# Two layers of self- and cross-attention on one core: when a group's row maxima are computed, and where its keys wait

## The reference

```python
h1 = ln(x);  x = attn(h1, h1,      20 heads of 16) + x      # self:  512 queries x  512 keys
h2 = ln(x);  x = attn(h2, context, 20 heads of 16) + x      # cross: 512 queries x 1601 keys
h3 = ln(x);  a, g = split(h3 @ ff_w1 + ff_b1)               # 320 -> 2 x 1280
x  = (a * gelu(g)) @ ff_w2 + ff_b2 + x
# attn: softmax(q k^T / 4) v per head, then a projection
```

## Time and profile before

| what | value |
|---|---|
| time, median of 3 runs | 3695.53 us (3688.76 to 3696.15) |
| time of the profiled execution | 3690.11 us |
| its span, first to last instruction | 3688.3 us |
| mean granted TensorE clock | 0.931 of full |
| busy: PE, DVE, ACT, POOL | 88%, 56%, 54%, 17% of the span |

### The profile page before, as it was taken

How to read it: one execution, slowest core, us unless ns; L and a number is a source line. 1 busy time by engine, 2 the same in 40 slices (tenths; PEclk the granted TensorE clock), 3 DMA queues, 4 the chain that set the end, 5 groups by cost and what they waited for, 6 DMA issues and landing times.

```text
span 3688.3 us, 43767 instructions
## 1 busy us (share of the span) xinstructions
PE 3235.1 (88%) x16320; PEld 1493.1 (40%) x16320; DVE 2080.8 (56%) x2565; ACT 1989.5 (54%) x3806; POOL 620.7 (17%) x676
## 2 busy tenths in 40 slices
PE   5887888998899989999899988999988988887877
PEld 2333333343353434534344433544344534433435
DVE  5555565665555765557555655556755665455511
ACT  1543565656655656456664566545665566354531
POOL 2231121203102120112202132021210031001001
PEclk8987988999998999999999888999999999998989
DMA  6434335333433243332443445323333243222202
GB/s 156 140 90 97 95 89 141 89 82 88 126 89 108 68 107 94 95 96 53 130 107 87 120 119 147 97 90 72 92 92 87 46 101 90 63 43 47 69 24 71
DMA packets 194515, 340.88 MB, mean 92 GB/s; under 512 B 19384, under 2 KB 101696, under 8 KB 193024
## 3 DMA queue, kind: packets, MB, share of 16 engines
q1 hardware_dynamic: 194304, 338.08, 35.5%
HBM read 202.29 MB, written 114.75 MB: 86 GB/s over the span
## 4 chain that ended last, share of the span: by engine, by line
PE 60%; DVE 14%; DMA 11%; ACT 6%; POOL 3%; issue 3%; SPq 3%; DVEq 0%; ACTq 0%; POOLq 0%
DVE mx L933 12%; PE pr L1124 11%; PE po L1141 11%; PE pd L1105 7%; PE pf L1049 5%; PE pf L996 5%; PE pf L1060 5%; DMA QS<-scr_q 5%; PE pf L1019 3%; PE pf L1037 3%; ACT ET L852 3%; PE pf L1028 3%; DMA scr_k<-HS 2%; PE pf L1052 2%; DMA raw<-ff_w_dram 1%
## 5 line engine op out<-in xcount | busy, mean ns | idle before, releaser
L852 ACT ACTIVATE ET<-pr 128x512 f32<-128x512 f32 (+1 forms) x2720 | 1478.1, 596 | 1372.5 <-PE pr L1124 1356.8
L933 DVE TENSOR_REDUCE mx<-pd 128x2 f32<-128x804 f32 (+2 forms) x1600 | 1569.4, 1033 | 1004.2 <-PE pd L1105 1001.7
L1124 PE MATMUL pr<-QS,KS 64*128 64x512 f32 (+1 forms) x2720 | 871.0, 514 | 86.6 <-ACT ET L852 84.1
L1105 PE MATMUL pd<-KS,QS 64*128 64x400 f32 (+2 forms) x3200 | 636.2, 396 | 160.0 <-DVE mx L933 85.4
L1141 PE MATMUL po<-ET,V 128*32 128x512 f32 (+2 forms) x5440 | 770.2, 640 | 1.2 <-ACT OU L858 1.2
L1124 PEld LDWEIGHTS pr<-QS,KS 64*128 64x128 f32 (+1 forms) x2720 | 337.4, 189 | 962.7 <-ACT ET L852 648.5
L1105 PEld LDWEIGHTS pd<-KS,QS 64*128 64x128 f32 x3200 | 361.1, 197 | 302.9 <-DVE mx L933 194.0
L743 POOL TENSOR_TENSOR HS<-uT,HS 128x512 fp32r<-128x512 f32 (+4 forms) x168 | 189.9, 1131 | 762.5 <-ACT uT L816 762.5
L759 POOL TENSOR_TENSOR OA<-OA,DEN 128x512 f32<-128x512 f32 (+1 forms) x48 | 60.8, 1267 | 1259.5 <-DVE DEN L941 1259.5
L1049 PE MATMUL pf<-HS,WS 128*128 128x512 f32 x730 | 217.7, 430 | 50.1 <-DVE uT L926 17.8
L1019 PE MATMUL pf<-cT,w_kv 96*128 96x400 f32 (+3 forms) x384 | 168.3, 564 | 31.5 <-ACT uT L816 30.6
(11 more groups left out here) (82 smaller groups left out, 2186.0 us busy)
## 6 DMA issues: line engine op xcount, KB each, us to landing
WS<-parts SPq DMA_DIRECT2D x160, 320.0 KB, 2.9
KS<-scr_k SPq DMA_DIRECT2D x80, 600.8 KB, 10.6
QS<-scr_q SPq DMA_DIRECT2D x80, 512.0 KB, 10.2
scr_k<-HS SPq DMA_DIRECT2D x144, 200.0 KB
scr_q<-HS SPq DMA_DIRECT2D x96, 256.0 KB
KS<-scr_k SPq DMA_DIRECT2D x80, 192.0 KB, 3.7
scr_k<-HS SPq DMA_DIRECT2D x48, 256.0 KB
OA<-OU SPq DMA_DIRECT2D x320, 32.0 KB
```

What stands on the lines that cost most here:

```text
L852: activation(ET[0:q.rows[k], s % 2, 2 * pair + e, :], pr[e][0:q.rows[k], :], ACT.Exp).then_inc(score_free, 1)
L933: v.reduce_max(mx[:, t, 2 * p:2 * p + 2, c], pd[no % 2][:, :, 0:cols], AX_X).then_inc(unit_free, 1)
L1105: ins = mm(pd[no % 2][:, e, 0:cols], queries[:, t * P:(t + 1) * P], keys, start=True, stop=True)
L1124: mm(pr[e][0:m, :], keys, queries, start=True, stop=True).then_inc(score_ready, 1)
```

## The change

It is one new plan for the units, with four parts around it.

1. **Units.** Outside the self-only stretches a group's units stand only on beats with `b % 4 == 2`, place three of a step. S units may spread over 16 beats in place of 8, so four places; C units have their own chain of `_turn`, so that S and C units may stand at one place. Per pair of 17 steps, 40 units: before, they stood at 17 places with two units and 6 with one. After, by the rule of the diff, the 510 steps of the mixed stretch have 262 places with two C units, 66 with three C, 117 with two S and then two C, 2 with two S and three C, 1 with two S, and 62 with none; the last 130 steps have 64 places with four C units, 8 with three, 3 with two, 55 with none. The first C group has four places with eight units; before it had eight with four.
2. **Slots and maxima by kind.** S groups stay in one slot of `QS`, C groups alternate between the other two; `mx` has a tile for each kind. A C group is loaded 16 beats earlier than before in the mixed stretch (with the end of the C group two before it), not together with an S group. Its first unit stands at least 11 beats behind the load, an S group's at least 8 (10 in effect); before it was 7 (8 in effect) for both. In the C-only stretch the load stays and the first unit stands 14 beats behind it, before it was 8.
3. **Self-only stretches.** Their units stay. Moves, reciprocals and division come earlier: 6, 9 to 12 and 13 beats behind a group's end. Fills of the second stretch begin up to one place earlier.
4. **Order of the last passes.** Fills of phase c = 6 are dealt by `deal_by_steps` (one stretch per step, two short ones at both odd places); `ff2` of pass 5 moves to the start of the last phase, where the norms `n3` are mixed with the values, and the last gate takes four `a` fills together, before three.
5. **Waits.** `turn_maxima` waits for all units issued before it, and the first unit behind a turn waits for the copies of that turn.

```diff
     elif c == N - 1:
-        first, rest = gate(c - 1, 3)
-        seq = places("v2b", c) + mixed(places("o2", c - 1), []) + places("n3", c - 1) + places("t3", c - 1)
-        seq += places("g", c - 1) + [first] + rest
+        first, rest = gate(c - 1, 4)
+        seq = places("ff2", c - 2) + places("o2", c - 1) + mixed(places("v2b", c), places("n3", c - 1))
+        seq += places("t3", c - 1) + places("g", c - 1) + [first] + rest
...
+        if i is None:
+
+            seq = [p for p in seq if p[0] != "ff2"]
...
+            _last = {s: max([p.end for p in GROUPS if p.slot == s], default=0) for s in range(SLOTS)}
+            _own = [p.slot for p in GROUPS if p.kind == _kind and (_kind == "C" or p.step0 >= 2 * G * TT)]
+            if _kind == "C" and _crosses >= 2:
+                _slot = _own[-2]
+            elif _kind == "S" and _own:
+                _slot = _own[-1]
+            else:
+                _slot = min(_last, key=_last.get)
...
-    _over = [p.n for p in GROUPS[:_q.n] if p.n <= _q.n - RING or p.shares_keys(_q)]
+    _over = [p.n for p in GROUPS[:_q.n] if p.slot == _q.slot or p.shares_keys(_q)]
...
 COPY, MOVE, INVERT, DIVIDE = 5, 8, (14, 15, 16, 17), 18
+
+MOVE_ALONE, INVERT_ALONE, DIVIDE_ALONE = 6, (9, 10, 11, 12), 13
...
+SHORT = ("t1", "t2", "t3", "tc")
+
+
+def deal_by_steps(stretches, steps):
+
+
+    slots, kinds = [], []
+    for stretch in stretches:
+        works = [p[0] for p in stretch if p[0] in STAGE]
+        if works and works[0] in SHORT and slots and kinds[-1] == works[0] and len(slots[-1]) == 1:
+            slots[-1].append(stretch)
+        elif slots and kinds[-1] is None:
+            slots[-1][-1] = slots[-1][-1] + stretch
+            kinds[-1] = works[0] if works else None
+        else:
+            slots.append([stretch])
+            kinds.append(works[0] if works else None)
+    assert len(slots) <= len(steps)
+    for k, slot in enumerate(slots):
+        for n, stretch in enumerate(slot):
+            PLACES.setdefault(4 * steps[k * len(steps) // len(slots)] + 1 + 2 * n, []).extend(stretch)
...
-        _behind = [b for b in _odd if b > 4 * _from + DIVIDE]
+        _behind = [b for b in _odd if b > 4 * _from + DIVIDE_ALONE + 2]
...
+    elif _c == N - 2:
+        deal_by_steps(_all, range(_from + 1, _to))
...
-    _from = max(_at + 7, _free, 0)
-
+
+    _alone = _q.end <= 2 * G * TT
+    _from = max(_at + (8 if _q.kind == "S" else 11), _turn[_q.kind] + 3, 0)
+    if _alone:
+        _from = max(_at + 7, _turn["S"] + 2, 0)
     _lag = 5 if 4 * _q.step0 - _from >= 24 else 3
-    _to = 4 * _q.step0 - _lag - (4 if _lag == 5 else 2)
+    _to = 4 * _q.step0 - _lag - 2
     if _q.kind == "S":
-        _to = min(_to, _from + 8)
-    _beats = [b for b in range(_from, _to) if b % 2 == 0]
+        _to = min(_to, _from + (8 if _alone else 16))
+    _beats = [b for b in range(_from, _to) if (b % 2 == 0 if _alone else b % 4 == 2) and b + 1 not in TURN_AT and b - 1 not in TURN_AT]
...
-        mx = sb("mx", [P, TT, HG, len(CHUNKS)])
+        mx = {"S": sb("mx1", [P, TT, HG, 1]), "C": sb("mx2", [P, TT, HG, len(CHUNKS)])}
...
-                if u == 0 and q.n:
-                    pe.wait_ge(max_copied, HG * q.n)
+                elif TURNS_BEFORE[no] > TURNS_BEFORE[no - 1]:
+                    pe.wait_ge(max_copied, HG * TURNS_BEFORE[no])
...
+            def turn_maxima(q, units):
+
+                pe.wait_ge(unit_free, units)
                 pe.wait_ge(max_steps, 3 * (q.n + 1))
```

More of the change, by code:

```diff
@@ L121, in stages_beside @@
             first, rest = gate(c - 1, 4)
-            seq += behind[:2] + places("t3", c - 1) + places("g", c - 1) + [first] + rest
-            behind = behind[2:]
+            seq += behind[:1] + places("t3", c - 1) + places("g", c - 1) + [first] + rest
+            behind = behind[1:]
+        if i is None:
+            seq = [p for p in seq if p[0] != "ff2"]
         if c + 3 < N:
-            behind = mixed(behind[:2], places("n1", c + 3)) + behind[2:]
+            behind = places("n1", c + 3) + behind
             behind += places("t1", c + 3) + places("q1", c + 3) + places("k1", c + 3)
@@ L136, with __init__ @@
 class Group:
-    def __init__(self, n, kind, i, g, step0, unit0, at):
+    def __init__(self, n, kind, i, g, step0, at, slot, uses):
         self.n, self.kind, self.i, self.g = n, kind, i, g
@@ L167 @@
                 _at, _selves = JP + T * (_selves % 3) if _c is None else 2 * JP, _selves + 1
-            GROUPS.append(Group(len(GROUPS), _kind, _pass, _g, _q.end if _q else 0,
-                                _q.unit0 + len(_q.units) if _q else 0, _at))
+            GROUPS.append(Group(len(GROUPS), _kind, _pass, _g, _q.end if _q else 0, _at, _slot,
+                                sum(p.slot == _slot for p in GROUPS)))
     PHASE_STEPS.append((_from, GROUPS[-1].end))
 STEP = [(q, k) for q in GROUPS for k in range(q.kt)]
-UNIT = [(q, u) for q in GROUPS for u in range(len(q.units))]
 LAST_OF = {(q.kind, q.i): q for q in GROUPS}
@@ L288, in split_for @@
     return max(fills, key=lambda p: SPLIT[p])
-STAGE_AT, UNITS_AT, TURN_AT, = {}, [0] * BEATS, {}
-_free = 0
+STAGE_AT, UNITS_AT, TURN_AT = {}, {b: [] for b in range(BEATS)}, {FIRST_BEAT: GROUPS[0]}
+_turn = {"S": FIRST_BEAT, "C": FIRST_BEAT}
 for _q in GROUPS:
@@ L462, in blocks_kernel @@
         gelu_done = sem("gelu_done")
-        staged = [sem(f"staged{r}") for r in range(RING)]
+        staged = [sem(f"staged{r}") for r in range(SLOTS)]
         unit_ready = sem("unit_ready")
@@ L693, in _ @@
                     set_scratch("q2", 1)
-                if ended(beat, MOVE):
-                    move_rows(ended(beat, MOVE))
+                if ended(beat, MOVE, MOVE_ALONE):
+                    move_rows(ended(beat, MOVE, MOVE_ALONE))
             sp.wait_ge(x_stored, 16 * B * TT)
@@ L763, in _ @@
                     beside(*p)
-                if ended_slot(beat, DIVIDE):
-                    divide(ended_slot(beat, DIVIDE))
+                if ended_slot(beat, DIVIDE, DIVIDE_ALONE):
+                    divide(ended_slot(beat, DIVIDE, DIVIDE_ALONE))
         @block.scalar
@@ L874, in _ @@
                     beside(*p)
-                if ended(beat, COPY):
-                    take_sums(ended(beat, COPY))
+                if ended(beat, COPY, COPY):
+                    take_sums(ended(beat, COPY, COPY))
         @block.vector
@@ L965, in _ @@
                     set_key_rows()
-                    for u in range(len(GROUPS[0].units)):
-                        reduce(GROUPS[0], u)
+                    for no in range(len(GROUPS[0].units)):
+                        reduce(no)
                 if beat in TURN_AT:
@@ L970, in _ @@
                 if 0 <= beat < BEATS:
[L971 to L975, removed]
+                    for no in range(UNITS_BEFORE[beat], UNITS_BEFORE[beat] + len(UNITS_AT[beat])):
+                        reduce(no)
+                for part, behind in enumerate(zip(INVERT, INVERT_ALONE)):
+                    if ended_slot(beat, *behind):
+                        invert(ended_slot(beat, *behind), part)
         @block.tensor
@@ L1149, in _ @@
                 if beat == FIRST_BEAT:
-                    for u in range(len(GROUPS[0].units)):
-                        unit(GROUPS[0], u)
+                    for no in range(len(GROUPS[0].units)):
+                        unit(no)
                 if beat in TURN_AT:
-                    turn_maxima(TURN_AT[beat])
+                    turn_maxima(TURN_AT[beat], UNITS_BEFORE[max(beat, 0)])
                 if 0 <= beat < BEATS:
@@ L1156, in _ @@
                         scores(s, r // 2)
-                    for no in range(UNITS_BEFORE[beat], UNITS_BEFORE[beat] + UNITS_AT[beat]):
-                        unit(*UNIT[no])
+                    for no in range(UNITS_BEFORE[beat], UNITS_BEFORE[beat] + len(UNITS_AT[beat])):
+                        unit(no)
                 if r == 3 and 1 <= s <= len(STEP):
```

70 lines of the change are left out of this document (39 added, 31 removed).

## The result

The changed kernel takes 4299.09 us (median of 4 runs, 4274.04 to 4335.67) against 3695.84 before: a ratio of 1.1635, 95% interval 1.1542 to 1.1728. That is 603 us more, where 270 were forecast, and above the range, which ended at 4130 us. The list under "The change" leaves two edits out: ahead of the transposes `t3` one fill of `v2a` stands in place of two, and the norms `n1`, which were mixed with the next two of these fills, now stand ahead of them. The profiled execution is the slowest of the four, 4335.67 us with a span of 4333.9 and a mean clock of 0.842, before 0.931.

A forecast was written before the change was run, and what follows sets the result against it. PE's order of issue was taken to set the pace, neither helper being full; +222 + 94 + 0 - 85 + 20 - 10 + 30 = +271 on 3690 gave 3961, forecast as 3965 us, range 3780 to 4130.

The forecast's parts named there:

- the waits for DVE: PE's unit matmuls would wait for DVE's `mx` for 400 to 550 us, before 85.
- the term for the clock: Long places, four in a row per pair: lower clock, 1 us for each of 30 pairs, +30 us, bounds 0 and 150.
- a clock below 0.90: Sign that the prediction is wrong: the granted clock falls below 0.90.
- Long places: Units at place three make PE wait for DVE's reduces: net +222 us in the mixed stretch, +94 in the cross-only one.
- Rival A: The clock falls with the long places, at a third of 183 places, 3 us each: 4115 us; chance 0.17.
- Loads: Earlier, separate loads of `QS` cut PE's waits and the clock loss around them: -85 us, bounds -40 and -110.
- Order of the last passes: `n3` covered by the values -9 us, `ff2` moved -1: together -10 us, bounds 0 and -25.
- Self-only stretches: Passes 0 and 1: DVE waits some 6 us for `DEN<-OU` on each of six slots, about half shows: +20 us.
- Rival B: PE's stall is covered in part, 120 us of other waits coming due during long places: 3845 us; chance 0.19.
- Rival C: A long place costs PE only its matmuls, only one of two waits remaining: about 3570 us; chance 0.11.

The follow-up runs named there:

- even-beat plan: The changed kernel with units on every even beat (places one and three) in all stretches, the rest as changed: 3779.68 us, ratio 1.0238 to the kernel before.

## Why the prediction was wrong

The direction and the waits for DVE were right, the size was not: +603 us for +270. The step that failed is the term for the clock. The prediction itself named a clock below 0.90 as the sign that it is wrong; it was 0.842. By its steps:

- *Long places.* Right at full clock: 4.77 us at the median for the 4.69 built, 4.28 for 4.09, 3.15 for 3.17 (three cross units in the mixed stretch), and PE's waits for `mx` were 404.7 us.
- *Clock, the term that was mis-sized.* It was put at +30 us, bounds 0 to 150. With PE's idle time in the long places filled by repeats the time falls by 277 us (some 36 either way), and some of the 2398 repeats cost time, so the clock's price is at least that. The term also counted the 30 pairs of the mixed stretch alone, while the cross-only stretch fell from 0.93 to 0.81 and took 840 us for the 740 forecast; with the clock back it takes 745. Rival A named it, at a third of the long places and 3 us each, and gave it 0.17 and 4115 us, too little in both. In the trace the clock stays down over whole neighbouring steps, with their fills and `weigh`, as the window of 36 us at 0.58 shows, and 145 of the 257 long places lie wholly or partly at half clock. The evidence was in the earlier trace rows, 30.8 us at 0.58 with DVE as the bound, and I set it aside because its fills were short and few.
- *Loads.* PE's waits for `QS` fell from 71.5 to 15.0 us, as forecast. What it gave in time wasn't measured alone.
- *The value fill ahead of `t3`* was not in the sum at all, nor in the list of the change: +31 us in the kernel before.
- *Reciprocals among the units* weren't either: perhaps +40 us, not clear of the noise. In the even-beat plan they cost more, some 60 us. I compared how many units stand on a beat, and not what else DVE's program has there.
- *Order of the last passes.* -10 forecast, -44 measured, outside its bounds. It was costed by one bare norm chain of the last phase; the phase before, where 25 us of the gain lie, was put at nothing for its new dealing and at 1 us for `ff2`.
- *Self-only stretches.* +20 forecast; the 40 steps take 281.9 us for 281.5, so nothing was lost there. DVE waited for `DEN<-OU` 6.6 us in four waits up to 350 us, where some 6 us on each of six slots were expected.
- *Rival B*, stalls that are covered: out, since 236 us less waiting gave 427 back. *Rival C*, only one of the two waits in a place: out, both are in the rows shown.

With the clock back, 4022.54 less 3692.38 are 330 us. The terms for it are 222 and 94 for long places, as built and not measured, 31 for the value fill, 40 for reciprocals and -44 for the order, 343 in all. What is left is near nothing, but it holds three things that no run parts: the gain of the loads (-85 forecast), the cost of the repeats, and a clock that is higher than before (0.948 for 0.931). So the sum fits without proving its terms.

## What to carry to other kernels

With two buffers between a producer and a consumer, be wary of giving the producer more than two pieces between other work, however idle the consumer is on average: here each piece more cost about one reduce of the consumer, 0.92 to 1.22 us. Cost short waits that an edit adds to TensorE twice, as waits and as slower work around them, and look in the old trace for a stretch that already looks like the new one. Before moving work to other beats, read what its consumer's program has on those beats: here the plan's empty beats were where the reciprocals are, and with even beats 17 places behind them cost some 60 us.

## What the runs showed of the hardware

- Issuing 2398 matmuls again, on top of 16320, took 6.4% off the kernel's time (4299.09 to 4022.54 us); the mean granted clock rose from 0.842 in the changed kernel's profiled execution to 0.948. The Trainium skill, page "TensorE: Matmul & The Clock Gate", section "A second HAM failure mode: psum-queue depth-cycling", has a kernel with such micro-idles swing between the clocks and lose throughput. By it rival A was the case, and the runs agree: the places of one form lie at either clock, 112 of 257 at full and 51 at half, and the time falls by 277 us when the idle time is filled.
- In the window of 36 us at a clock of 0.58 PE is shown busy for 29.75 us. Its busy share hides a low clock, since at half clock its matmuls fill the time.
- No single wait of PE in the half-clock place shown was above 0.90 us, and none in the window of 36 us above 1.09; in this kernel the clock fell with many short waits and no long one.
